# A recommendation tower with a two-layer cross network on one core: four wide groups of x instead of three, in 2 KB packets

## What is computed

```python
z0 = einsum('bid,bjd->bdij', x0, x0).reshape(B, D, F0 * F0)
cur0 = relu(einsum('bdk,kl->bld', z0, W0))            # 1521 -> 128
next_h, direct0 = split(cur0, 2, axis=1)              # 64 and 64
z1 = einsum('bid,bjd->bdij', x0, next_h).reshape(B, D, F0 * 64)
cur1 = relu(einsum('bdk,kl->bld', z1, W1))            # 2496 -> 128
z = sum(concatenate([direct0, cur1], axis=1), axis=-1)
h = relu(concatenate([z, dense_ctx]) @ W_top1 + b_top1); h = relu(h @ W_top2 + b_top2); y = h @ W_top3
```

## Time and profile before

| | |
|---|---|
| median of three runs | 449.84 us |
| the profiled execution | 449.96 us |
| its span, first to last instruction | 448.1 us |
| PE busy | 405.8 us, 91% |
| DVE busy | 347.6 us, 78% |
| ACT busy | 227.2 us, 51% |
| POOL busy | 270.8 us, 60% |
| mean granted clock of PE | 0.970 |
| DMA traffic | 64.03 MB, mean 143 GB/s |

### The profile page before, as it was taken

One profiled execution on the slowest core, in us unless ns is written; L12 is line 12 of the kernel. 1 busy time (PEld: TensorE's weight loads), 2 busy tenths in 40 slices (PEclk: granted clock), 3 DMA queues, 4 the chain that ended last, 5 costly groups with the idle time before them and its releaser, 6 DMA issues.

```text
span 448.1 us, 4257 instructions
## 1 busy us (share of the span) xinstructions
PE 405.8 (91%) x1446; PEld 238.8 (53%) x1446; DVE 347.6 (78%) x197; ACT 227.2 (51%) x224; POOL 270.8 (60%) x180
## 2 busy tenths in 40 slices
PE   0263299999999999999999999999999999999997
PEld 0221056565656565656565565656565656565744
DVE  0301676998989898989898989899898989998900
ACT  2122346556464646465564655655646464645413
POOL 5777888888888888888888888888810000000000
PEclk9958589999999999999999999999999999999999
DMA  8369269493959495868668596959493949752000
GB/s 286 97 152 182 43 145 186 108 213 84 216 117 216 100 205 107 198 136 196 133 155 171 138 193 143 188 125 208 98 211 84 218 96 212 165 129 59 1 0 0
DMA packets 25740, 64.03 MB, mean 143 GB/s; under 512 B 8512, under 2 KB 16661, under 8 KB 19446
## 3 DMA queue, kind: packets, MB, share of 16 engines
q1 hardware_dynamic: 19128, 60.55, 60.4%
q0 software_dynamic: 5632, 1.35, 3.2%
q10 hardware_dynamic: 958, 1.86, 1.2%
HBM read 59.87 MB, written 3.84 MB: 142 GB/s over the span
## 4 chain that ended last, share of the span: by engine, by line
PE 87%; issue 8%; SPq 4%; DMA 0%; ACT 0%
PE acc L495 22%; PE acc L525 14%; PE acc L517 13%; PE acc L518 13%; PE acc L533 12%; PE sums L485 5%; PE spread L506 3%; PE spread L562 2%; SPq L243 1%; SPq L232 1%; SPq L195 1%; SPq L221 0%; PE sums L551 0%; PE sums L553 0%; SPq L205 0%
## 5 line engine op out<-in xcount | busy, mean ns | idle before, releaser
L282 POOL DMA_INDIRECT found<-in_table_dram,rows_sb x176 | 270.6, 1538 | 56.6 <-issue 53.0
L423 DVE TENSOR_TENSOR z_lo<-z,z_hi 128x2048 fp32r<-128x2048 f32 x64 | 146.2, 2285 | 2.3 <-ACT z_hi L325 1.3
L325 ACT ACTIVATE z_hi<-z 128x2048 fp32r<-128x2048 f32 x64 | 122.3, 1911 | 16.8 <-DVE z L415 15.0
L415 DVE TENSOR_TENSOR z<-x_wide,h 128x2048 f32<-128x2048 f32 x48 | 109.8, 2288 | 12.5 <-ACT h L309 8.7
L495 PE MATMUL acc<-squares,w 128*128 128x512 f32 x224 | 114.7, 631 | 0.0
L517 PE MATMUL acc<-z_hi,w_hi 128*128 128x512 f32 x256 | 106.9, 417 | 0.7 <-ACT cur L318 0.7
L518 PE MATMUL acc<-z_hi,w_lo 128*128 128x512 f32 x256 | 100.3, 392 | 0.0
L301 ACT ACTIVATE squares<-sums 128x1024 f32<-128x1024 f32 x64 | 58.8, 919 | 78.7 <-PE sums L485 70.7
L525 PE MATMUL acc<-z_lo,w_hi 128*128 128x512 f32 x256 | 90.5, 475 | 0.0
L415 DVE TENSOR_TENSOR z<-spread,h 128x2048 f32<-128x2048 f32 x32 | 73.1, 2283 | 1.3 <-PE spread L506 1.2
L525 PEld LDWEIGHTS acc<-z_lo,w_hi 128*128 128x128 f32 x256 | 47.0, 188 | 32.3 <-issue 26.8
(11 more groups left out here) (41 smaller groups left out, 111.2 us busy)
## 6 DMA issues: line engine op xcount, KB each, us to landing
x_wide<-x_rows SPq DMA_DIRECT2D x96, 512.0 KB
x_parts<-x_rows SPq DMA_DIRECT2D x62, 64.0 KB
found<-in_table_dram,rows_sb POOLq DMA_INDIRECT x176
w_sb<-in_w_dram SPq DMA_DIRECT2D x1, 1280.0 KB, 7.2
x_rows<-found_hi SPq DMA_DIRECT2D x32, 26.8 KB
x_rows<-found SPq DMA_DIRECT2D x32, 26.8 KB
x_rows<-found_lo SPq DMA_DIRECT2D x30, 26.8 KB
z<-in_select_dram ACTq DMA_DIRECT2D x1, 576.0 KB, 7.9
```

What stands on the lines that cost most here:

```text
L282: pool.indirect_dma_start(out=found[:, b, s * D:s * D + D], out_offset=None, in_=table, in_offset=bass.IndirectOffsetOnAxis(ap=rows_sb[:, ...
L325: nc.scalar.activation(z_hi[:, n % RING], z[:, n % RING], ACT.Copy).then_inc(hi_done, 1)
L415: nc.vector.tensor_tensor(z[:, n % RING], x, h[:, c % 2, :].unsqueeze(1).to_broadcast([P, QUADS, N]), ALU.mult).then_inc(multiplied, 1)
L423: nc.vector.tensor_tensor(z_lo[:, n % RING], z[:, n % RING], z_hi[:, n % RING], ALU.subtract).then_inc(lo_done, 1)
```

## The change

Group 1 joins `WIDE`, and PE spreads group 3 alone. There are now four widens for each chunk, with a buffer of its own for each group. In `x_wide` the four rows of a partition are no longer neighbours: each has 8 unused numbers behind it, so that a DMA writes four pieces of 2 KB, 2080 bytes apart, instead of one of 8 KB. The groups take other features: the halves of a wide group may lie anywhere in the 39 rows, some features are read twice, and `layout` leaves the weights of the second copy at zero. At the start, SP issues two widens of chunk 0, then `bring(1)`, then the other two, then `bring(2)`. A spread-out no longer waits for the other one of its chunk.

```diff
--- before.py
+++ after.py
@@ -31,6 +31,8 @@
 
 
 QUADS = 4
+
+PAD = 8
 QF = 16
 QSTART = [0, 16, 7, 23]
 
@@ -44,10 +46,10 @@
 
 G = 5
 T1 = G * QUADS
-SPREAD = [1, 3]
-WIDE = [0, 2, 4]
-SPREAD_FROM = [0, 24, 12, 36]
-WIDE_FROM = [[4, 8], [16, 20], [28, 32]]
+SPREAD = [3]
+WIDE = [0, 1, 2, 4]
+SPREAD_FROM = [12, 16, 14, 37]
+WIDE_FROM = [[0, 4], [8, 18], [22, 26], [30, 33]]
 
 VT = (G - 1) * QUADS
 VG = G - 1
@@ -98,7 +100,7 @@
         found_hi = sb("found_hi", [GP, BUFS, GW], F32R)
         found_lo = sb("found_lo", [GP, BUFS, GW], F32R)
         x_rows = nc.dram_tensor("x_rows", (BUFS, 3, F, N), F32, kind="Internal")
-        x_wide = sb("x_wide", [P, len(WIDE), QUADS * N])
+        x_wide = sb("x_wide", [P, len(WIDE), QUADS, N + PAD])
         x_parts = sb("x_parts", [P, BUFS, N], F32R)
 
         select_sb = sb("select_sb", [P, T0 + len(SPREAD), P], F32R)
@@ -229,9 +231,9 @@
                 if c:
                     sp.wait_ge(multiplied, G * (c - 1) + WIDE[i] + 1)
                 for a, f in enumerate(WIDE_FROM[i]):
-                    sp.dma_start(x_wide[HALF * a:HALF * a + HALF, i, :],
-                                 x_rows[b, 2, f:f + QUADS, :].rearrange("f n -> (f n)").unsqueeze(0)
-                                 .to_broadcast([HALF, QUADS * N])).then_inc(wide_in[i], 16)
+                    sp.dma_start(x_wide[HALF * a:HALF * a + HALF, i, :, 0:N],
+                                 x_rows[b, 2, f:f + QUADS, :].unsqueeze(0).to_broadcast([HALF, QUADS, N])
+                                 ).then_inc(wide_in[i], 16)
 
             sp.dma_start(ids_sb[:, :], ids).then_inc(ids_in, 16)
             sp.dma_start(w1_sb[:, :, :], w1).then_inc(w1_in, 16)
@@ -256,9 +258,11 @@
             lay_out(sp, 0, 0)
             place(sp, 0, [0, 1])
             full_rows(0)
-            for i in range(len(WIDE)):
-                widen(0, i)
+            widen(0, 0)
+            widen(0, 1)
             bring(1)
+            widen(0, 2)
+            widen(0, 3)
             bring(2)
             for c in range(CHUNKS - 1):
                 for i in range(len(WIDE)):
@@ -407,7 +411,7 @@
                     x = spread[:, :, :]
                 else:
                     dve.wait_ge(wide_in[WIDE.index(g)], 32 * (c + 1))
-                    x = x_wide[:, WIDE.index(g), :].rearrange("p (t n) -> p t n", n=N)
+                    x = x_wide[:, WIDE.index(g), :, 0:N]
                 if n >= RING and is_v(n - RING):
                     dve.wait_ge(lo_done, v_count(n - RING))
                 elif n >= RING:
@@ -499,8 +503,8 @@
             def spread_out(n):
 
                 c, i = n // G, SPREAD.index(n % G)
-                if c or i:
-                    pe.wait_ge(multiplied, G * c + SPREAD[i - 1] + 1 if i else G * (c - 1) + SPREAD[-1] + 1)
+                if c:
+                    pe.wait_ge(multiplied, G * (c - 1) + SPREAD[i] + 1)
                 for q in range(QUADS):
                     rows = slice(32 * q, 32 * q + 32)
                     last = nc.tensor.matmul(spread[:, q, :], select_sb[rows, T0 + i, :], x_parts[rows, c % BUFS, :],
@@ -660,7 +664,10 @@
     for i, g in enumerate(WIDE):
         for a in range(2):
             f = WIDE_FROM[i][a]
-            w1[HALF * a:HALF * a + HALF, QUADS * g:QUADS * g + QUADS] = from_w1[f:f + QUADS].transpose(1, 0, 2)
+            for k in range(QUADS):
+
+                if a == 0 or f + k >= WIDE_FROM[i][0] + QUADS:
+                    w1[HALF * a:HALF * a + HALF, QUADS * g + k] = from_w1[f + k]
 
     def by_tile(a):
         return np.ascontiguousarray(a.reshape(T0, P, -1).transpose(1, 0, 2))
```

## The result

493.48 us against 449.89, each the median of four runs on the same chip (492.80 to 494.59 and 449.59 to 450.14). The ratio is 1.0973, with a 95% interval of 1.0952 to 1.0994: slower by about 10%. The profiled execution took 493.13 us with a span of 491.3, so the span grew by 43.2 us from 448.1.

A forecast was written before the change was run, and what follows sets the result against it. It took PE as the bound, before and after, with the DMA loop just hidden. Span 448.1 - 7.0 (PE) - 4.5 (start) = 436.6 us, so 438.5 as profiled, 438 against the median; range 433.5 to 464.

The forecast's parts named there:

- the DMA loop: SP's queue, per chunk: widens, rows, parts, next widens; 5.1 + 4 x 4.5 = 23.1 us, just hidden under PE's 23.21.
- Wide group, 4.5 us: SP's queue: one wide group of 1.05 MB taken at 4.5 us, from the parts' 233 GB/s in 2 KB pieces.
- the upper bound of 4.97: Time in us of one wide group if 1.05 MB still moves at 211 GB/s, as before the change.
- Fixed part, 5.1 us: SP's loop without wide groups: 1.2 us to full rate, 1.3 for rows to land, 2.6 for issuing parts.
- The first rival: DMA loop becomes the bound: wide groups stay at 4.97 us, loop 25.0 us, time 456 us; chance 0.38.
- the lead: First widen issued 11.8 us before its product and needing about 6.2, so some 5 us are absorbed once.
- PE, -7.0 us: One spread-out fewer on PE per chunk, 16 x 0.44 = 7.0 us gained, bounded by 5.3 to 8.0.
- DVE, nothing: Group 1's product on DVE reads `x_wide` in place of PSUM: 2288 against 2283 ns, so no cost.
- The start, -4.5 us: Chunk 1's split at 36, PE restarting 5.6 us earlier; 4.5 us gain taken, with 0 and 8 as ends.
- chunk 3's gather: At the start, named late next: ACT wants it 2.4 us after POOL; a lag like 8.2 would eat the gain.
- the lag: From chunk 1's last gather on POOL to ACT's use: 8.2 us before, assumed 2.5 with fewer groups ahead, smaller pieces.

The follow-up runs named there:

- the middle layout: Changed kernel with each wide group's second feature in partitions 32 to 95, the first in 0 to 31 and 96 to 127, three DMAs per group: 457.76 us, ratio 1.0169.
- the old order: Changed kernel with all four wide groups of chunk 0 issued ahead of chunk 1's rows and parts, as before the change: 491.19 us, ratio 1.0936.

## Why the prediction was wrong

**The step that failed is the DMA loop, "5.1 + 4 x 4.5 = 23.1 us against PE's 23.21: just hidden".** Both of its terms were too small. By the windows and SP's timeline of one loop of 26.6 us:

| term | predicted | measured |
|---|---|---|
| first widen's issue to full rate | 1.2 | 1.8 (203.23 to 205.0) |
| four wide groups | 18.0 | 19.7 (205.0 to 224.7) |
| rows behind them, data and landing | 1.3 | 2.2 (224.7 to 226.89) |
| issue of the parts, to the next widen | 2.6 | 3.0 (226.89 to 229.85) |
| loop | 23.1 | 26.7 (26.62 from issue to issue) |

- *Wide group, 4.5 us.* It is 4.9, all but the upper bound of 4.97. I had put the value between bounds by the row that looked nearest, the parts, because they share the size of the pieces. The experiment with three groups in 2 KB shows that this size does next to nothing (218 GB/s). The one with 128 partitions points to the partitions: 353 GB/s for the same bytes in the same pieces, though from four rows in place of eight. The parts are four DMAs to four quarters of the partitions, and a busy share of 0.49 over 2.4 us is too short and mixed a stretch to price 15 us of another transfer by. The page "SBUF — State Buffer" (Door 1: The DMA port swizzle) of the Trainium skill gives the half of the ports that 64 partitions reach as the reason. The traces agree with it at 209 to 218 GB/s for halves against 353, and the 317 in parts of the middle layout fit too. A count of ports alone does not say why two halves under way at once stayed at 209; no run here shows that.
- *Fixed part, 5.1 us.* It is 7.0. Its pieces were read where the queue was idle: the landing from chunk 0, for the last row DMA alone. In the loop all nine DMAs of rows stand behind the burst, so their own 1.0 us of data counts as well. This term alone, with 4.5 for a group, makes 25.0 and would have turned the forecast over.
- *The first rival* had the mechanism, and each of its signs came true (waits for `x_parts` and `x_wide`, 211 to 218 GB/s in a burst), and it was priced at 456. Its loop was 25.0 and is 26.8; over 13 loops that is 23 us more. It also counted 4.5 us gained at the start where 6.4 were lost, 11 us more. 456 + 23 + 11 = 490, which leaves 3 us; the 5 us for the lead were right (4.6). I had set the range by groups of up to 5.1 us and had left the fixed part at one value, so 493 lay far outside it. In a loop that runs 13 times both terms were short, together by 3.6 us, and that is 47.
- *PE, -7.0 us.* Right in kind, and more than priced: with the transfers fast enough, a chunk takes 22.95 where I had 23.21. In the changed kernel it changes nothing, since PE waits.
- *DVE, nothing.* Right: 2290 against 2283 ns.
- *The start, -4.5 us.* Wrong in sign: 6.4 us lost by the first loop. The split of chunk 1 came at 40.33 (36 predicted) and PE restarted 2.8 us earlier, not 5.6:

```profile
40.33 0.35 ACT L298 ACTIVATE found_hi<-found 117x176 fp32r<-117x176 f32 x1 [4.68 <-DMA found<-in_table_dram,rows_sb]
...
49.64 0.80 PE L489 MATMUL sums<-x_parts,select_sb 64*128 64x512 f32 x2 [12.05 <-DMA x_parts<-x_rows]
...
60.56 0.35 ACT L298 ACTIVATE found_hi<-found 117x176 fp32r<-117x176 f32 x1 [9.06 <-DMA found<-in_table_dram,rows_sb]
```

  And two of POOL's gathers for chunk 2:

```profile
42.00 3.03 POOL L286 DMA_INDIRECT found<-in_table_dram,rows_sb  x1 [0.30 <-issue]
45.33 4.69 POOL L286 DMA_INDIRECT found<-in_table_dram,rows_sb  x1 [0.30 <-issue]
```

  The split at 60.56 is what is late next, and I had it one chunk too far out. Not chunk 3's gather but chunk 2's comes late, and it holds ACT for 9.06 us, to 60.56 where the split was at 54.19. The rows of chunk 2 and all later transfers move back by 6.4 us. The new order is not all of it. On POOL the last gather of chunk 2 ended at 53.93 where it was 49.04, and with the old order it was 53.70, again with one gather of 4.68 us; that kernel issued the first widen of chunk 1 at 63.80. So 3.0 of the 6.4 us are lost in either order, and 3.4 go with the order. At the start the prediction had no term for longer gathers on POOL; why they grow is not shown. The page "DMA: Bandwidth & Descriptors" of the Trainium skill (Queues, rings and completion order) tells of turns between queues; that the lag would shrink much with 2 KB pieces was my own conclusion. It shrank by 0.6 to 0.7 us: 7.5 for 8.2 with three groups, 6.4 for 7.0 with four (the split at 40.33 beside 40.91). I had counted on 5.7. It was short beside a shorter burst, as in the kernel with 128 partitions: 2.3 us, with the split at 36.20.

**What stays open.** Why a small transfer in one queue takes 5.6 to 7.6 us to land beside a burst in another, and why two halves from two queues stay at 209 GB/s together, is not explained by any run here. And the 55 us between 64 and 128 partitions was measured with other features in the upper half; a layout that gets 353 GB/s with the right ones was not found; the middle one reaches 251.

## What to carry to other kernels

Before a transfer is added to a queue that also feeds itself (rows out, parts in, widens behind), write down the loop from one issue to the same issue of the next chunk, with every DMA's data and landing in it, and multiply the error of each term by the number of turns. Here the loop was priced 3.6 us (13%) too short, so one that came out 0.1 us under PE's pace was not hidden; with three groups the loop by measured terms, 7.0 + 14.9 = 21.9 us against 23.65, was. Price a transfer by a row with the same partitions, not the same piece size. If the loop is too long, give part of the bytes to a second queue so that it works while the first waits for its round trip; that raised no rate here and still turned 1.10 into 0.99.

## What was unexpected of the hardware

- A transfer to 64 partitions ran at 209 to 218 GB/s, to all 128 at 353 in the same 2 KB pieces. Two halves from two queues at the same time stayed at 209, and three pieces with the middle 64 partitions as one of them went up to 317.
- The parts in another queue than the burst, 0.26 MB, landed 5.6 to 7.6 us after the last issue beside a burst in the other queue, as against 2.3 us without one. Gathers were late too, by 6.4 to 8.2 us from POOL's last one to the split, with pieces of 2 KB and of 8 KB; beside the shorter burst of the 128-partition DMAs it was 2.3.
- Pieces 2 KB long and 2080 bytes apart made no difference (0.9994) where the transfers are hidden; in the changed kernel 8 KB in one piece were 3 us quicker.
